# A graph network on one core: the columns that TensorE fetches spread 0, 2, 2, 2 over the groups of a trip, equal sources repaired in three operations, and the end of the first pass in another order

## The reference, cut to what matters

```python
agg = segment_sum(x[src], dst)                 # L0 and L1 (GIN): plain sums
m   = relu(concat(h[src], h[dst], ef) @ W1 + b1) @ W2 + b2
agg = segment_sum(m, dst)                      # L2: three message layers, with a GRU
e   = leaky_relu(a_s[src] + a_d[dst])          # L3: two attention layers
w   = exp(e - segment_max(e, dst)[dst])
out = segment_sum(w / z[dst] * h[src], dst)
```

## Time and profile before

| | us |
|---|---|
| median of 3 runs (2414.42 to 2416.88) | 2416.3 |
| the profiled execution's own time | 2421.36 |
| its span, first to last instruction | 2419.6 |
| busy in the span: PE / DVE / POOL / ACT | 1919.1 / 1819.6 / 1634.3 / 1098.6 |
| mean granted TensorE clock | 0.883 of full speed |

### The profile page before, as it was taken

How to read it: one execution, slowest core, us unless ns; L and a number is a source line. 1 busy time by engine, 2 the same in 40 slices (tenths; PEclk the granted TensorE clock), 3 DMA queues, 4 the chain that set the end, 5 groups by cost and what they waited for, 6 DMA issues and landing times. The chain is left out here.

```text
span 2419.6 us, 48584 instructions
## 1 busy us (share of the span) xinstructions
PE 1919.1 (79%) x15773; PEld 1553.5 (64%) x15773; DVE 1819.6 (75%) x6739; ACT 1098.6 (45%) x2756; POOL 1634.3 (68%) x1641
## 2 busy tenths in 40 slices
PE   4989567999599898589897589895779994789951
PEld 3877436888358786258786268774358883578841
DVE  7999844887248999559999569999437776367775
ACT  1435223444124444234443324443438886378873
POOL 5777554777657767477767577776467775777763
PEclk9999757999699999699998799997869996699985
DMA  7989915997237999358998258997156775267751
GB/s 224 329 300 352 289 52 179 334 356 255 63 100 263 302 297 299 104 154 267 298 300 283 79 188 295 301 296 234 32 115 201 227 228 160 27 216 230 219 158 41
DMA packets 308197, 522.96 MB, mean 216 GB/s; under 512 B 105947, under 2 KB 141349, under 8 KB 307748
## 3 DMA queue, kind: packets, MB, share of 16 engines
q1 hardware_dynamic: 236256, 437.07, 53.4%
q0 software_dynamic: 52160, 52.25, 10.4%
q10 hardware_dynamic: 19588, 31.50, 3.9%
HBM read 353.76 MB, written 166.87 MB: 215 GB/s over the span
## 5 line engine op out<-in xcount | busy, mean ns | idle before, releaser
L1842 PE MATMUL ps<-big 128*128 128x256 f16 (+1 forms) x13038 | 1527.2, 277 | 89.5 <-DMA big<-kept 62.0
L1842 PEld LDWEIGHTS ps<-big 128*128 128x128 fp8e5 x13038 | 1282.0, 99 | 301.4 <-issue 109.4
L743 POOL DMA_INDIRECT ringG<-tab,src_i x1137 | 1116.3, 982 | 412.1 <-issue 327.3
L1272 DVE SCALAR_TENSOR_TENSOR ringG<-ringG,same 128x64 f32<-128x64 f32 x2075 | 583.2, 281 | 46.4 <-DMA ringG<-tab,src_i 14.2
L844 ACT ACTIVATE ringG<-big 128x512 uint8<-128x512 uint8 (+1 forms) x684 | 367.4, 626 | 4.3
L1272 DVE SCALAR_TENSOR_TENSOR edge_side<-edge_side,same 128x64 f32<-128x64 f32 x1245 | 347.2, 279 | 1.6
L874 ACT ACTIVATE ringG<-ringG 128x512 f32<-128x512 f32 x156 | 97.9, 628 | 459.8 <-DVE ringG L1354 459.8
L1244 DVE COPY_PREDICATED ringG<-twins,ringG 128x128 uint32<-128x128 int32 (+2 forms) x798 | 240.1, 301 | 75.3 <-ACT ringG L844 74.7
L1394 DVE SCALAR_TENSOR_TENSOR ringG<-ringG,expo 128x65 f32<-128x65 f32 x830 | 237.6, 286 | 75.2 <-ACT ringG L885 12.7
L743 POOL DMA_INDIRECT ringG<-in_x,src_i x188 | 205.8, 1095 | 103.7 <-issue 51.2
L832 ACT ACTIVATE big<-ps 128x512 int32<-128x512 f32 (+1 forms) x228 | 124.3, 587 | 257.9 <-PE ps L1842 257.6
(11 more groups left out here) (274 smaller groups left out, 1471.2 us busy)
## 6 DMA issues: line engine op xcount, KB each, us to landing
big<-kept SPq DMA_DIRECT2D x156, 768.0 KB
sums<-ringG SPq DMA_DIRECT2D x260, 256.0 KB
edge_side<-ef_mix SPq DMA_DIRECT2D x156, 256.0 KB
edge_side<-q_at_start SPq DMA_DIRECT2D x156, 256.0 KB, 5.2
big<-kept SPq DMA_DIRECT2D x78, 480.0 KB
big<-kept SPq DMA_DIRECT2D x78, 384.0 KB
sums_w<-ringG SPq DMA_DIRECT2D x104, 264.0 KB
kept<-big SPq DMA_DIRECT2D x26, 768.0 KB, 8.0
```

Of the source, the lines that this page charges most:

```text
L743: return pool.indirect_dma_start(out=out_ap, out_offset=None, in_=table, in_offset=bass.IndirectOffsetOnAxis(ap=index, axis=0))
L1272: return v.scalar_tensor_tensor(now, before if u == 0 else source[:, (u - 1) * D:u * D], same[:, c:c + 1], now, ALU.mult, ALU.add)
L1842: mm = pe.matmul(ps[:, bank_of(k, i, m), 0:2 * n] if wide else to, hot[t][:, u * P:(u + 1) * P], opener[:, 0:2 * n] if wide else split[:, ...
```

## The change

`FULL` becomes (0, 2, 2, 2): a trip's groups have 8, 2, 2, 2 cold columns, 14 as before; chunk m now belongs to group m + 1. The first group with a hot column is now the second of a trip, so ScalarE's `evict` moves by one group, to ahead of group 4i's `clip` or `weigh` (behind group 4i-1's). `twin_piece` no longer goes by chunks: three operations a trip cover all six units (384 words a row, 396 in attention; 256 or 264 in the last trip), and the first of them waits until all chunks of the trip are placed. They stand where `fix_between` puts them for group 4i+1: in the loop of group 4i in `pooled_trip` and `message_pass`, in that of 4i-1 in attention. `FEW` goes: trip 11 of a message pass fetches six units like the others (three columns fewer by GpSimd, 25 matmuls more). `make_twins`, which makes the masks in pass 0, has three operations fewer.

In pass 0, `load_first` moves in SP's order behind all four groups of trip 10. The two wide rows get a semaphore of their own, `span_rows_in`; VectorE waits after trip 11 for `nxt` alone, raises `prep_done` after `start_i`, runs trip 12, and only then waits for the wide rows and makes `spans`, for which TensorE waits (`spans_made`) ahead of "gin0".

```diff
@@ -149,12 +149,12 @@
 
-FULL = (1, 1, 2, 2)
+FULL = (0, 2, 2, 2)
 UMAX = sum(FULL)
...
 COPIES = [(1, 2), (0, 1), (0, 2)]
-GROUPS_OF = [range(0, 2), range(2, 3), range(3, 4)]
+GROUPS_OF = [range(1, 2), range(2, 3), range(3, 4)]
 
@@ -202,12 +202,11 @@
 ALL, HOT, LAST = Hot(FULL), Hot(FULL), Hot((0, 0, 2, 2))
-FEW = Hot((0, 1, 2, 2))
 BIT_OF, ODD, MATCHED, SHOWN = (0x01, 0x10, 0x20), 4, (0x05, 0x50, 0xA0), 0x62626262
...
 TO_INT = 32768.0
-UNITS = [(HOT, HOT, LAST), (HOT, HOT, LAST)] + [(HOT, FEW, LAST)] * NLAYER + [(HOT, HOT, LAST), (HOT, HOT, LAST)]
+UNITS = [(HOT, HOT, LAST)] * 7
 PASSES = [Pass(k, *UNITS[k], D if k < 5 else WG) for k in range(7)]
@@ -437,7 +436,7 @@
         first_ready, first_out, first_in = sem("first_ready"), sem("first_out"), sem("first_in")
-        prep_done = sem("prep_done")
+        prep_done, span_rows_in, spans_made = sem("prep_done"), sem("span_rows_in"), sem("spans_made")
         pens_ready, pens_turned = sem("pens_ready"), sem("pens_turned")
@@ -617,7 +616,7 @@
 
-            def trip(k, i, l=None, after_first=None):
+            def trip(k, i, l=None):
                 for j in range(GROUPS):
@@ -632,8 +631,6 @@
                             load_codes(i + 3, j)
-                    if after_first is not None and j == 0:
-                        after_first()
 
@@ -671,10 +668,11 @@
                 row = first_d.rearrange("n o -> (n o)")
-                sp.dma_start(FM[1], row[0:NP].partition_broadcast(P)).then_inc(first_in, 16)
-                sp.dma_start(FM[6], row[1:NP + 1].partition_broadcast(P)).then_inc(first_in, 16)
-
-            trip(0, FIRST_AT + 1, after_first=load_first)
+                sp.dma_start(FM[1], row[0:NP].partition_broadcast(P)).then_inc(span_rows_in, 16)
+                sp.dma_start(FM[6], row[1:NP + 1].partition_broadcast(P)).then_inc(span_rows_in, 16)
+
+            trip(0, FIRST_AT + 1)
+            load_first()
             for i in range(FIRST_AT + 2, TRIPS):
@@ -1148,7 +1146,7 @@
                 by_group = src_i[:].rearrange("p (i j c) -> p i j c", j=GROUPS, c=COLS)
-                for j in range(GROUPS):
+                for j in range(1, GROUPS):
                     h, at = FULL[j], sum(FULL[:j])
@@ -1224,46 +1222,39 @@
 
-            def twin_piece(k, i, m, x):
+            def twin_piece(k, i, x):
 
                 way, unit = PASSES[k], PASSES[k].unit(i)
-                w, js, us = way.width, unit.groups_of(m), unit.of_chunk(m)
+                w, us = way.width, unit.us
                 if x == 0:
-                    v.wait_ge(placed, CHUNKS_BEFORE[k] + way.before(i) + unit.chunks.index(m) + 1)
+                    v.wait_ge(placed, CHUNKS_BEFORE[k] + way.before(i + 1))
                 else:
                     v.wait_ge(vchain, taken[0])
-                s0, h, rows = slot_of(k, i * GROUPS + js[0]), FULL[js[0]], ringG[:].bitcast(U32)
+                s0, rows = slot_of(k, i * GROUPS), ringG[:].bitcast(U32)
 
                 def columns(which):
-                    at = unit.start(js[0], which) * w
-                    if len(js) > 1:
-                        return rows[:, s0:s0 + len(js), at:at + w]
-                    return rows[:, s0, at:at + h * w].rearrange("p (h d) -> p h d", h=h)
+                    at = unit.start(unit.first, which) * w
+                    return rows[:, s0 + unit.first:s0 + GROUPS, at:at + 2 * w].rearrange("p j (h d) -> p j h d", h=2)
 
                 to, of = COPIES[x]
-                taken[0] = chain.mark(v.copy_predicated(
-                    columns(to), twins[:, x, i, us[0]:us[-1] + 1].unsqueeze(2).to_broadcast([P, len(us), w]), columns(of)))
-
-            def chunk_of_group(k, g):
-
-                if g >= NG:
-                    return None
-                unit, j = PASSES[k].unit(g // GROUPS), g % GROUPS
-                return next((m for m in unit.chunks if unit.groups_of(m)[0] == j), None)
+                flags = twins[:, x, i, us[0]:us[-1] + 1].rearrange("p (j h) -> p j h", h=2).unsqueeze(3).to_broadcast(
+                    [P, len(us) // 2, 2, w])
+                taken[0] = chain.mark(v.copy_predicated(columns(to), flags, columns(of)))
+
+            def opens_unit(k, g):
+
+                return g < NG and g % GROUPS == PASSES[k].unit(g // GROUPS).first
 
...
 
-                m = chunk_of_group(k, g)
-                if m is not None:
+                if opens_unit(k, g):
                     for x in range(len(COPIES)):
-                        twin_piece(k, g // GROUPS, m, x)
+                        twin_piece(k, g // GROUPS, x)
 
...
 
-                if u in (3, 5, 7):
-                    m = chunk_of_group(k, g)
-                    if m is not None:
-                        twin_piece(k, g // GROUPS, m, (u - 3) // 2)
+                if u in (3, 5, 7) and opens_unit(k, g):
+                    twin_piece(k, g // GROUPS, (u - 3) // 2)
 
@@ -1557,7 +1548,7 @@
 
-            v.wait_ge(first_in, 48)
+            v.wait_ge(first_in, 16)
             link(v.tensor_tensor(has[:], nxt[:], first[:], ALU.is_gt))
@@ -1567,11 +1558,13 @@
             link(v.tensor_tensor(tmp[:], tmp[:], first[:], ALU.add))
-            link(v.tensor_copy(start_i[:], tmp[:]))
-
+            v.tensor_copy(start_i[:], tmp[:]).then_inc(prep_done, 1)
+
+            pooled_trip(0, 12)
+
+            v.wait_ge(span_rows_in, 32)
             link(v.tensor_scalar(FM[1], FM[1], tail[:, 0:1], None, ALU.is_le))
-            v.scalar_tensor_tensor(spans[:], FM[6], tail[:, 1:2], FM[1], ALU.is_gt, ALU.mult).then_inc(prep_done, 1)
-            pooled_trip(0, 12)
+            v.scalar_tensor_tensor(spans[:], FM[6], tail[:, 1:2], FM[1], ALU.is_gt, ALU.mult).then_inc(spans_made, 1)
 
@@ -1942,6 +1935,7 @@
             pe.wait_ge(summed, NG)
+            pe.wait_ge(spans_made, 1)
             run_wave("gin0", {"l0_carry": carries(last_row_of(0)), "l0_T": turn(yN),
```

## The result

The changed kernel takes 2475.75 us (median of 5 runs, 2468.11 to 2476.71), the kernel before 2416.3: a ratio of 1.0245, 95% interval 1.023 to 1.0259. Forecast were 2463, in 2436 to 2492. The profiled execution of the changed kernel took 2476.71, its span is 2474.8: 55.2 more than the 2419.6 before. The medians are 59.5 apart; the profiled execution of the kernel before was 5 us above its median, that of the changed kernel 1.

The account below looks back on a forecast made before the run. VectorE hardly idles in pass 0 and message passes; in attention no engine is full and the timeline decides. Terms -5 - 5 + 0 + 4 + 53 = +47 take 2421.36 to 2468, median 2463 us, range 2436 to 2492.

Parts of the forecast that it names:

- The wait in attention: In attention, VectorE waits 3.38 us a trip for all chunks; trips go from 17.7 to 20.34, +53 us in all.
- The wait in a message pass: In message passes, VectorE waits 0.88 us a trip for all chunks; trips 20.47 against 20.37, +4 us over three passes.
- The trio's price: Equal-source operations in a message trip: one wide trio costs 1.63 us instead of 2.40 for three, at 1.08 ns a word.
- TensorE hides its longer idle stretch: In attention, longer idling costs TensorE 1.65 us of clock; its 19.4 stays under the 20.34 trip, so costed at nothing.
- the rival in which TensorE bounds: In attention, late evictions make TensorE lose 1.65 us two or three times a trip; about 2510, chance 0.08.
- Pass 0 and its end: Pass 0 saves 0.77 us a trip, -5 net; last sum 10 earlier, TensorE gains 5 at its end; pass 1 0.

Follow-up runs that it names:

- experiment with copies by chunk: Changed kernel with three copies a chunk in attention again, each trio waiting for its own chunk, eviction left where the change put it: 2423.54 us, ratio 1.0026.
- three kernels below: Changed kernel with eviction one group earlier in passes 2 to 6 (2412.34 us), with attention copies by chunk (2423.54), or with earlier message and split attention eviction (2395.2).

## Why the prediction was right, point by point

The mechanism was right, and the forecast of 2463 came out 13 us low; most of that is the one term of pass 0.

- **The wait in attention** was right in place, size and consequence: 3.38 worked out, 3.40 measured; a trip of 20.34, measured 20.48; +53, measured +55. The experiment with copies by chunk takes 50.6 of it away. One reading of it was incomplete: that TensorE's 17.04 and 0.68 make today's trip of 17.7 holds for pass 5, but in pass 6 GpSimd's gathers, back to back, allow no less than 234 either.
- **The wait in a message pass** was right: 0.88 worked out, 0.77 measured; trips of 20.47, measured 20.39. The three passes came out 4 shorter and not 4 longer, since the full trip 11 and the last trip together run some 2 us faster than before; the stretches ahead of them grew by 5.5, so that +1.5 is left of the +4.
- **The trio's price** was right: 588 ns for 384 words, 575 by the 1.08 ns a word; 1.64 us for the three in a message trip, 1.63 worked out.
- **TensorE** hides its longer idle stretch, as said, but by less than was worked out. Its clock fell to 0.95 from 1.00 in attention. Where it did, a trip's matmuls took 1.6 to 2.8 us more, against the 1.65 of the prediction; with 0.7 us of idle time left in the tightest trip, the rival in which TensorE bounds was nearer than worked out.
- **Pass 0 and its end** is the term that was mis-sized: -10 worked out, with pass 1 at 0, and -0.4 measured at the end of pass 1 (-1.4 to -3.2 in the traces of three kernels below whose first two passes are the same). Four steps of it failed. A trip of pass 0 saves 0.1 to 0.3, not 0.77. The last sum comes 5.9 earlier, not 10: no gather waited any more for a store behind `load_first` and the last gather ended 9.0 earlier, but VectorE waited 15.2 us in all for gathers to land. TensorE then gains 0.5, not 5. And pass 1 is not the 0 it was put at: its first gather begins 2.8 earlier, but its 188 gathers, one after the other without a wait, take 241.2 us instead of 238.7 (239.9 to 241.5 in every kernel with the new columns, 238.6 and 238.7 with the old). Why single gathers are a little longer with the new columns was not tried.
- **Not in the prediction:** the first group of a pass now needs eight gathers, not five, and VectorE waits for them. At the start of pass 4 this is 2.8 of the 4.6 us in the table:

```profile
1437.24 0.69 DVE L1343 TENSOR_TENSOR ringG<-ringG,edge_side 128x512 f32<-128x512 f32 x1 [9.19 <-DMA ringG<-tab,src_i]
```

  The first gather began at 1423.17, so 14.1 to this; in the kernel before 1424.24 to 1435.53, 11.3. Ahead of passes 2 and 3 the stretch grew by 0.4 and 0.5 only; what covers it there was not looked into.

## What to carry to other kernels

Joining operations that each waited for a part of some work into one that waits for all of it moves the first wait to the last part's time; before doing so, work out on one timeline when the last part is there and when it is asked for. Where it is late, the producer's place in its own engine's program is the lever: here one group earlier gave 21 us in the message passes, and parting the eviction around a `weigh` brought pass 5 to 223.1 us, under the 229.0 before. Before an operation's issue is blamed for a late transfer, check whether anything that is waited for stands behind it: here the held stores were needed by no gather of the pass. A transfer that is moved to another queue to free one engine can still hold what travels beside it: `nxt` landed 22.5 us after its issue beside the wide rows, 12.6 without them.

## What was not expected of the hardware

While SP's store of `first`, 3,200 single words, was under way (issued at 256.95, waited for until 276.8 in the changed kernel), the DMA engines were busy and moved little. Their share and GB/s are the last two columns, in the changed kernel:

```profile
240.00:256.00 16.00, 15.36 (x136) 13.01 (x134) 15.15 (x45) 7.96 (x18) 12.54 (x12) 1.00 1.05 394
262.00:276.00 14.00, 3.13 (x13) 1.93 (x14) 10.42 (x33) 1.56 (x3) 8.79 (x9) 0.50 1.21 78
```

The kernel before has the same stretch, with 70 GB/s. TensorE was busy for 3.13 of the 14 us, and the gathers of group 44 landed 14 us after the last of them was issued; this is the wait of 6.10. The stretch comes ahead of the wide rows, which are issued from 277.25 on. That the single words cause it fits the times, but no run left them out.

`nxt`, 3,200 single words read back, landed 12.6 us after its issue with no wide rows on their way and 22.5 beside both of them from ScalarE's queue; on SP's queue, with the wide rows behind it, it took 6.8 and 8.0 with the old end of pass 0 and some 14 with the new one. So the wide rows are not all that makes it late. The first wide row held SP for 4.7 to 13.0 us in the eight traces in which SP issues it, each time until 0.9 to 1.7 us before `nxt`, ahead of it in that queue, had landed; from ScalarE's queue its issue took 0.33 and 0.38. That points at `nxt` more than at the wide row. Which resource they share was not shown.
